# A gated cross-attention and mixture-of-experts block: the second batch's context in a buffer of its own, and the first softmax's centring shared between two engines

## The reference

```
query, key = ctx @ Wq.T + bq, ctx @ Wk.T + bk          # ctx: 512 x 256 a batch, q and k: 512 x 128
attention  = softmax(query @ key.T)                    # 512 x 512
x = x + tanh(g0) * (layernorm(x) mixed by attention)   # einsum bln,bmn->blm
h = layernorm(x)
x = x + tanh(g1) * (h + shared(h) + top-2 of 8 experts(h))
```

## Time and profile before

| | |
|---|---|
| median of 3 runs | 316.96 us (314.45 to 317.94) |
| profiled execution | 318.51 us |
| its span in the trace | 316.8 us |
| TensorE busy | 293.5 us, 93% |
| VectorE busy | 214.0 us, 68% |
| ScalarE busy | 131.9 us, 42% |
| GpSimd busy | 140.2 us, 44% |

### The profile page before, as it was taken

How to read it: one execution, slowest core, us unless ns; L and a number is a source line. 1 busy time by engine, 2 the same in 40 slices (tenths; PEclk the granted TensorE clock), 3 DMA queues, 4 the chain that set the end, 5 groups by cost and what they waited for, 6 DMA issues and landing times.

```text
span 316.8 us, 5646 instructions
## 1 busy us (share of the span) xinstructions
PE 293.5 (93%) x1593; PEld 208.0 (66%) x1607; DVE 214.0 (68%) x580; ACT 131.9 (42%) x236; POOL 140.2 (44%) x163
## 2 busy tenths in 40 slices
PE   8598959999999999999999999899999999999990
PEld 3246737787787767877888788566666666665730
DVE  0757788658775538876886588467776767676094
ACT  3237257930656843463724651243434343433000
POOL 3702988175740185086078355024434343434200
PEclk9959999999999999999999999999999999999997
DMA  7999399611224011000992992334343434339598
GB/s 232 364 231 262 102 188 188 254 70 67 66 104 164 0 69 67 0 0 7 193 233 71 176 228 97 89 85 127 103 134 103 130 108 122 114 89 305 168 370 332
DMA packets 30492, 46.01 MB, mean 145 GB/s; under 512 B 2880, under 2 KB 20032, under 8 KB 30464
## 3 DMA queue, kind: packets, MB, share of 16 engines
q1 hardware_dynamic: 19888, 27.66, 28.5%
q0 software_dynamic: 10432, 17.99, 24.5%
q10 hardware_dynamic: 144, 0.00, 0.0%
HBM read 39.58 MB, written 14.72 MB: 171 GB/s over the span
## 4 chain that ended last, share of the span: by engine, by line
PE 71%; issue 9%; DVE 8%; POOL 6%; ACT 2%; DMA 2%; DVEq 0%; SPq 0%; POOLq 0%; ACTq 0%
PE bank L750 15%; PE bank L493 11%; PE bank L494 11%; PE bank L495 11%; PE bank L767 8%; POOL xg L428 5%; PE bank L505 4%; PE bank L488 4%; PE bank L740 3%; PE bank L758 2%; PE bank L628 1%; DVE prob L1076 1%; DVE acc L1434 1%; DMA xg<-lnb,slot 1%; POOL hT_lo L417 1%
## 5 line engine op out<-in xcount | busy, mean ns | idle before, releaser
L477 POOL DMA_INDIRECT z<-ysb,dest x39 | 37.2, 955 | 62.4 <-DVE ysb L1410 62.1
L1018 ACT ACTIVATE sigc<-bank 128x352 f32<-128x352 f32 x39 | 18.1, 463 | 54.2 <-PE bank L750 54.2
L1405 DVE TENSOR_TENSOR hrow<-sigc,bank 128x352 bf16<-128x352 f32 x39 | 20.3, 521 | 23.9 <-ACT sigc L1018 23.9
L428 POOL DMA_INDIRECT xg<-lnb,slot x32 | 31.7, 991 | 9.9 <-issue 7.3
L750 PE MATMUL bank<-wgu_lo,xTb 128*128 x156 | 36.0, 313 | 0.0
L750 PE MATMUL bank<-wgu_hi,xTb 128*128 x156 | 36.0, 312 | 0.0
L493 PE MATMUL bank<-lnT_hi,sgu_lo 128*128 128x512 f32 (+2 forms) x72 | 29.6, 411 | 1.6 <-DVE lnT_lo L1113 1.6
L767 PE MATMUL bank<-wd_sb,hTb 128*128 (+1 forms) x104 | 29.0, 381 | 1.1 <-issue 0.4
L1410 DVE TENSOR_SCALAR ysb<-bank,wt 128x512 bf16<-128x512 f32 x39 | 29.1, 747 | 1.0 <-PE bank L767 0.9
L495 PE MATMUL bank<-lnT_hi,sgu_hi 128*128 128x512 f32 (+2 forms) x72 | 28.4, 395 | 0.0
L494 PE MATMUL bank<-lnT_lo,sgu_hi 128*128 128x512 f32 (+2 forms) x72 | 28.3, 394 | 0.0
(11 more groups left out here) (186 smaller groups left out, 658.2 us busy)
## 6 DMA issues: line engine op xcount, KB each, us to landing
xt<-xg SPq DMA_DIRECT2D x39, 129.0 KB
xT_raw<-xT SPq DMA_DIRECT2D x4, 1024.0 KB, 7.3
acc<-x SPq DMA_DIRECT2D x4, 1024.0 KB, 9.5
out<-acc SPq DMA_DIRECT2D x16, 256.0 KB, 3.9
wgu_lo<-wguT POOLq DMA_DIRECT2D x2, 1408.0 KB, 13.3
wgu_hi<-wguT POOLq DMA_DIRECT2D x2, 1408.0 KB, 14.0
cx<-ctxT SPq DMA_DIRECT2D x4, 512.0 KB, 4.6
wd_sb<-wdT POOLq DMA_DIRECT2D x2, 1024.0 KB, 10.8
```

The source lines that it names most:

```text
L428: nc.gpsimd.indirect_dma_start(out=xg, out_offset=bass.IndirectOffsetOnAxis(ap=slot[:, c, j:j + 1], axis=0), in_=lnb[c][:, j, :], in_offse ...
L477: nc.gpsimd.indirect_dma_start(out=z, out_offset=bass.IndirectOffsetOnAxis(ap=dest[:, u:u + 1], axis=0), in_=ysb[:, r, :], in_offset=None) ...
L1018: act.activation(sigc[:, v, :], bank[2 * v][:, 0:I], ACT.Sigmoid).then_inc(s["csig"], 1)
L1405: V.tensor_tensor(hrow[:, v, 0:I], sigc[:, v, :], bank[2 * v + 1][:, 0:I], ALU.mult).then_inc(s["ch"], 1)
```

## The change

It has three parts.

1. ctx(1) gets a tile of its own, `cx1`, in the place of `sig`, which is first written much later. Its load has its own semaphore and stands ahead of x(0). SyncE's wait for `proj` falls away, so that `sgu_raw`, `sd_raw` and the padding writes are issued without a wait too. `load_ctx(2)` still goes into `cx`.
2. Probability tiles 0 and 1 of batch 0 are centred by ScalarE (`normalise(0, 0)` and `normalise(0, 1)`, which stand before `soft(0, 2)` and `soft(0, 3)`), and tiles 2 and 3 by VectorE, which waits until the tiles before are centred (`prb`). VectorE's list keeps the row maxima and the reciprocals, and all four `prob_low` come after `centred(3)`; ScalarE's four `prob_high` come after `soft(0, 3)`.
3. TensorE starts the first two energy tiles with the matmuls that need only q_hi, q_lo and k_hi, and adds those with k_lo when that is there. `project(1, 0)` moves ahead of the four `turn_prob(0, j)`, `project(1, 1)` behind them.

The transfers:

```
+        (cx1,), cx1_end = place((("cx1", [P, CT, L], F32),), hT_end)
+        assert cx1_end <= sig_end
...
             def load_ctx(b):
-                sp.dma_start(cx[:], ctxT[b].rearrange("(k p) l -> p k l", p=P)).then_inc(s["ctx_in"], 16)
+                dst, done = (cx1, "ctx1_in") if b == 1 else (cx, "ctx_in")
+                sp.dma_start(dst[:], ctxT[b].rearrange("(k p) l -> p k l", p=P)).then_inc(s[done], 16)
...
             load_xT(0)
+            load_ctx(1)
             load_x(0)
-            sp.wait_ge(s["proj"], 2)
-            load_ctx(1)
```

TensorE (`project(1, n)` now waits for `ctx1_in` and reads `cx1`):

```
             project(0, 1)
+            pe.wait_ge(s["qhi"], 2)
+            pe.wait_ge(s["qlo"], 1)
+            for j in range(2):
+                tok = slice(j * P, (j + 1) * P)
+                pe.matmul(energy_bank(0, j)[:, :], q_lo[:, tok], k_hi[:], start=True, stop=False)
+                pe.matmul(energy_bank(0, j)[:, :], q_hi[:, tok], k_hi[:], start=False, stop=False)
+            pe.wait_ge(s["qlo"], 2)
+            for j in range(2):
+                tok = slice(j * P, (j + 1) * P)
+                pe.matmul(energy_bank(0, j)[:, :], q_hi[:, tok], k_lo[:], start=False, stop=True).then_inc(s["eng"], 1)
+            energy(0, 2)
+            energy(0, 3)
+            project(1, 0)
+            pe.wait_ge(s["const"], CONSTS)
             for j in range(LT):
-                energy(0, j)
-            pe.wait_ge(s["const"], CONSTS)
-            turn_prob(0, 0)
-            project(1, 0)
-            turn_prob(0, 1)
+                turn_prob(0, j)
             project(1, 1)
-            turn_prob(0, 2)
-            turn_prob(0, 3)
```

ScalarE:

```
             soft(0, 1)
+            normalise(0, 0)
             soft(0, 2)
-            prob_high(0, 0)
+            normalise(0, 1)
             soft(0, 3)
-            prob_high(0, 1)
-            prob_high(0, 2)
-            prob_high(0, 3)
+            for j in range(LT):
+                prob_high(0, j)
```

VectorE, `centred` and the list:

```
                 dve.wait_ge(s["rden"], j + 1)
+                dve.wait_ge(s["prb"], j)
...
             over_sum(0, 0)
-            centred(0)
             row_max(0, 2)
             over_sum(0, 1)
-            centred(1)
             row_max(0, 3)
             over_sum(0, 2)
             centred(2)
-            prob_low(0, 0)
             over_sum(0, 3)
             centred(3)
-            prob_low(0, 1)
-            prob_low(0, 2)
-            prob_low(0, 3)
+            for j in range(LT):
+                prob_low(0, j)
```

More of the change, by code:

```diff
@@ L209, in gated_block @@
         s = {n: sem(n) for n in (
-            "ctx_in w_in small_in sgu_in sd_in wgu_in wgu2_in wd_in const gates split_hi split_lo "
+            "ctx_in ctx1_in w_in small_in sgu_in sd_in wgu_in wgu2_in wd_in const gates split_hi split_lo "
             "stat1 var1 rstd1 stat2 var2 rstd2 coef ln2 proj qhi qlo t2 lnThi lnTlo xThi xTlo probT probTlo eng nmax expd rden prb tp "
@@ L497, in project @@
             def project(b, n):
-                pe.wait_ge(s["ctx_in"], 16 * (b + 1))
+                if b == 1:
+                    pe.wait_ge(s["ctx1_in"], 16)
+                else:
+                    pe.wait_ge(s["ctx_in"], 16 * max(b, 1))
                 if b == 1:
@@ L504, in project @@
                 for k in range(CT):
-                    mm = pe.matmul(bank[QK_BANK + n][:, :], wqk_sb[:, k, n, :], cx[:, k, :], start=(k == 0), stop=(k == CT - 1))
+                    mm = pe.matmul(bank[QK_BANK + n][:, :], wqk_sb[:, k, n, :], (cx1 if b == 1 else cx)[:, k, :], start=(k == 0), stop=(k == CT - 1))
                 mm.then_inc(s["proj"], 1)
```

## The result

| | before | after |
|---|---|---|
| median of 8 runs, same chip | 315.65 us (314.45 to 317.94) | 313.89 us (313.34 to 314.66) |
| profiled execution | 318.51 us | 314.28 us |
| its span | 316.8 us | 312.5 us |

What follows compares the result with a forecast made beforehand. The kernel was taken as bound by TensorE's matmuls and its waits. Starting mix(0) 5.55 us earlier takes the profiled 318.51 to 313.0; the median lying 1.55 lower gives 311.4 us, range 310.0 to 315.3.

Steps and rivals of the forecast that it cites:

- Mechanism: Before the first turn: VectorE's centred(0) takes 3.16 us instead of 0.49 because it is held during GpSimd's xT_lo.
- The sum to mix(0), 5.55 us: From the first energies to the start of mix(0): all steps together move that start from 26.45 to 20.9.
- the median of 316.96 lies 1.55 lower, which gives 311.4: Whole kernel: from the profiled 318.51 less 5.55, 313.0, to a median 1.55 us lower.
- The clock falls all the same: Rival, turns between 14.5 and 19.0 us: TensorE drops to half speed, mix(0) at 22.9, gain 3.5, 313.5 us; chance 0.22.
- Transfers: Load queue: xT(0) not delayed, xT(1) hardly moved; rival with xT(0) up to 2.6 us late, 314.0 us, chance 0.09.
- later than 10: Sign of a wrong forecast: GpSimd's cast, which had started at 9.64 us, starts after 10.
- The shared port pair: VectorE and GpSimd: one holds the ports a whole instruction, so a late xT(0) delays centred(2) one to one.
- The forecast of `centred(2)`: VectorE, from 15.55 us: about 0.9 us long, held, ending 0.3 us behind xT_lo at 16.45.
- Not carried: Rival, behind mix(0): overdrawn small slacks or other waits take gain back, leaving 0 to 3 us, 315.5 us; chance 0.15.
- slower: Rival, load queue served side by side: xT(0) lands at 22, mix(0) starts 2.1 us later than before, 319 us; chance 0.04.
- the split energies: TensorE's first energies: start at k_hi, 9.71, instead of k_lo, 10.50; first tile ready at about 11.2, 0.3 us earlier.

Runs made afterwards that it cites:

- gpsimd_waits: Kernel before, except that GpSimd starts xT_lo of batch 0 only when all four tiles are centred; 315.95 us against 317.88 beside it, ratio 0.9917 to 0.9988.
- before_again: Kernel before, unchanged, measured and profiled again on another chip; 318.64 us against 318.63 beside it, ratio 0.9979 to 1.0054.
- after_third: Changed kernel, unchanged, measured and profiled a third time; 314.39 us against 317.68 for before, ratio 0.9897.
- after_mid_filled: Changed kernel with project(1, 1) between turns 1 and 2 and 9 filler matmuls in the wait of energy(1, 2); 312.09 us, 0.9853 of before.
- after_again: Changed kernel, unchanged, measured and profiled a second time; 313.71 us against 318.63 for before, ratio 0.9867.
- only_centring: Kernel before with only the ScalarE and VectorE part of the change (tiles 0 and 1 centred on ScalarE); 315.10 us against 318.63, ratio 0.9902.

## Why the prediction was right, and where it was off

- *Mechanism.* Right. `centred(0)` was held by GpSimd's xT_lo: gpsimd_waits shows 0.49 us for it, after shows 0.81 for ScalarE's centring beside the same instruction. Part 2 alone carries most of the gain, 0.9902 against 0.9867 for the whole change.
- *The sum to mix(0), 5.55 us.* Right against the profile it was made on: 26.45 to 20.91 is 5.54. That it is right to 0.01 us is luck, since errors cancelled. The start was 0.67 us late (k_hi at 9.69 instead of 9.02, since the projection weights landed 4.4 us behind their issue instead of 3.8). Three steps made that up. Nothing held `centred(2)` by then, as xT_lo was done at 16.12 when it came at 16.26, so turn 2 was only 0.53 late. Turns 2 and 3 took 1.07 us up to the start of the projection where 1.25 was summed. And `mix(0)` started 1.56 us after `project(1, 1)` did, where 1.9 was summed: the 1.87 us are its length to its modelled end, and the next matmul started before that.
- *"the median of 316.96 lies 1.55 lower, which gives 311.4".* This step failed. It takes a difference between two profiled executions and subtracts it from a median. Some 3.0 us of the 26.45 were the half-speed stretch of that execution: before_again has 23.47 with the same gap. With the clock held on both sides up to `mix(0)`, the change moves it from 23.47 to 20.91, 2.6 us; with the clock fallen in before alone, 5.5. The 2.6 is on the low side, because before_again had its projections earlier: counted from k_hi (8.74 and 9.69) it is 14.73 us against 11.22, 3.5 us. The measured difference of the medians was 1.8 us on the first chip, 4.9 and 3.3 us on the two where the changed kernel was repeated; by the ratios it was 2.1, 4.2 and 3.3. Those two medians of before are 3.0 and 2.0 us above the first chip's; the changed kernel's are 0.2 below and 0.5 above. It would be easy to say that before loses the clock more often there, but the record doesn't show it: on those two chips the mean clock of before (0.984 and 0.986) is about that of the changed kernel beside it (0.984 and 0.984). The gain of 4.2 and 3.3 us there was had at about the same mean clock. On the first chip the changed kernel had 0.989, and no clock is on record for the runs of before. Why its before was so fast there, and its gain smaller, is open.
- *"The clock falls all the same", 0.22, 313.5.* It lies nearest to the 313.89 measured, but the first trace doesn't show what it says, a fall before 24 us. Under-weighted all the same. I argued from one stretch of 9 us that held its clock with a gap of 2.04 us. In three traces of after the clock fell within 18 to 19 us in two and within 36 to 37 in the third. Its price was somewhat high: 1.3 and 1.4 us (2.2 with the hold of 0.75) from `project(1, 0)` to `mix(0)`, against the 2.0 that I had. And the falls behind `mix(0)`, at 36 and at 42, had no price in the sum at all.
- *Transfers.* Right in the first trace. xT(0) was there at 9.59 in after (9.64 before) with 3 MB more queued behind it. By the ring order that the Trainium skill states in "DMA: Bandwidth & Descriptors", section "Queues, rings and completion order", it should be, and this trace agrees. A small delay is not excluded: GpSimd's cast starts at 8.34 to 10.12 in the eight traces with the new load order and at 8.46 to 9.89 in the five with the old, and "later than 10", a sign of being wrong, came in three of the eight, after_third among them. xT(1) landed some 2.7 us before it was asked for (16.21 + 13.5 = 29.7 against 32.40), and in all thirteen traces ScalarE's xT_hi waited for TensorE.
- *The shared port pair.* By the rule of "SBUF — State Buffer" in the Trainium skill, section "SBUF: two separate sides", the later of the two engines waits for the whole instruction of the other. `centred` at 3.16, 1.41 and 0.49 us, by how much of xT_lo was left, agrees, and so does its end 0.28 us behind xT_lo. The forecast of `centred(2)`, about 0.9 us and held, was not met in the first trace (0.49), but it was in after_mid_filled (0.94), and exceeded in after_third.
- *Not carried, slower.* The first did not happen as a wait; the profiled pair keeps 5.0 us at 60 us (hT_hi of the shared expert, 60.12 and 55.12), 4.9 at VectorE's last sums (301.53 and 296.66) and 4.3 at the end of the span. Slower did not happen.
- *Parts 1 and 3.* The text gave them 0.3 us for the split energies and counted their place in the sum without asking what they are worth alone: nothing that was measured (0.9961 to 1.0027). On top of part 2 they seem to be worth more: from k_hi (9.69 and 9.38) to `mix(0)` it is 11.22 us against 12.51, both at full clock. after_again has 313.71 and only_centring 315.10 us beside the same before, but the intervals of their ratios overlap, so in the time this is not shown.

## What to carry to other kernels

A profile is one execution. Where it shows a half-speed stretch of TensorE behind a gap, work out the stretch at full clock as well and keep both sums, because the next execution may hold the clock there and lose it at the next thin place. When two engines share a gap in the trace, look for an instruction that takes several times its usual duration: it may be held, which its end just behind the other engine's instruction gives away, and moving it to an engine that is not held can be worth the whole hold. Real work moved into a gap (`project(1, 1)` between the turns) cost nothing here, and in both traces that have it the clock held.

## What the runs showed of the hardware

The clock of one program differs from execution to execution: before fell at 15 us once, behind a gap whose whole length was 3.02 us, and once only at 39, with a gap of 3.25 at 13 to 16. In two traces of after it fell behind gaps of 1.43 and 2.17 us with thin work around them, and in the first, behind one of 1.42 us in the same place, it did not. The first loads landed at different times too: k_hi started between 8.74 and 9.81, GpSimd's cast of xT(0) between 8.3 and 10.1, and through the hold of VectorE that moves the end of the stretch. Within one program the slower executions are those with the lower mean clock: over the twelve runs of each of seven kernels it is 1.6 to 2.5 us for each hundredth. And the spread of the runs shrank with the gaps, from 5.8 us (before) to 1.9 us (after_mid_filled, in fewer runs: 6 against 23).
